# Second attention of a two-layer block: scores on two halves of TensorE's rows, and VectorE's steps without PSUM moved to GpSimd

## The chip, the cores and the metric

The kernel runs on one core of a Trainium2 chip, as one program. The metric is the device time of a whole execution in microseconds (us), the median over several runs. The engines are named PE (TensorE; its weight loads are PEld), DVE (VectorE), ACT (ScalarE), POOL (GpSimd) and SP (SyncE, which here issues most of the DMAs).

## The reference

The reference is two transformer layers on x of shape 32 x 256 x 128, each a sum of the stream, an attention and a feed-forward part. The change touches only the attention and the router of the second layer, which for one batch item (T = 256 tokens, C = 128) come to this:

```
Q, K, V = x @ wq, x @ wk, x @ wv                    # 16 heads of 8
local  = window attention, blocks of W = 32 queries, 2W = 64 keys, causal inside the window
GQ, GK, GV = x @ wgq, pool(x @ wgk), pool(x @ wgv)  # 8 latent heads, 64 pooled latents (4 tokens each)
rem    = softmax(GQ GK^T / sqrt(8), masked) @ GV @ r_out_w
out    = (sigmoid(Q gl) * local + sigmoid(Q gr) * rem) @ w_out
probs  = softmax(x @ gate_w); w, idx = top_8(probs); w = w / sum(w)   # router of the experts
```

## The kernel before, in words

The program goes through five stages: layernorm and first attention over 32 batches of 256 tokens, the first feed-forward part with tokens sorted by expert, then the second attention with the router, and last the experts. The stage of the second attention handles one batch (`Batch(pair, half)`, `.b` its number) at a time. Each engine has its own queue, written out by hand in a function `step1`, and runs it strictly in order; semaphores (`S[...]`) link the queues. Names in `step1`: `b` is the batch in work, `p` the one before, `n` the next, `m` the one after that. Buffers are double, so at any moment parts of four batches are under way.

For a batch the steps run as follows. POOL fetches rows of the first feed-forward result by an indirect DMA (`gather`), multiplies them by the gate and adds them to the stream (`stream1`), and normalises (`norm1`, which waits in its middle for DVE's mean and variance, `mean1`). PE transposes (`xt1`), ACT copies the transposed tile to SBUF (`xT1`). DVE sums four tokens at a time into the pooled latents (`pool_latents`), and ACT spreads them (`xp1`). PE makes queries, keys and router logits (`qk`), latent queries and keys (`latents`), values. ACT writes the queries and keys into masked layouts (`keys`, `latent_keys`).

The scores of a batch come in four groups g of two blocks each. For a group PE (`scores`) puts 12 score tiles of 64 columns into two PSUM banks, one for each block n: a bf16 matmul of the identity with a mask, and on top of it the fp32 scores, with all 128 rows of the array in use though each head group lives on 32 of them. DVE takes the maximum and subtracts it (`shift`), ACT takes the exponential (`soft`), DVE transposes 32 x 32 blocks (`turn`), PE multiplies by the values (`attend`). After the four groups ACT copies the sums of the exponentials (`dens`) and then the unnormalised rows out of PSUM (`attended`), DVE inverts the sums (`invert1`), POOL multiplies the rows by them (`normalise_rows`, semaphore `scaled`), DVE transposes them (`turn_rows`), PE multiplies the remote part by its weight (`remote`). In the next `step1`, with the batch now called `p`, DVE forms the two gated parts (`combine`, `at1` and `at2`) and their sum `aT`, PE multiplies by `w_out` (`project`), and DVE adds the result to the residual (`finish`).

The router runs beside it on DVE: the top eight logits (`route`), then the weights of the experts and the shared gate (`weigh`: mask, sum, reciprocal, `sgc`, product into `tab`), which SP writes out.

Of the kernel before, what the change touches and what calls it, by code (L numbers as in the profile page):

```python
# [33 lines left out]
def program(nc, a, out):  # L34
# [27 lines left out]
    with ctx:  # L62
# [21 lines left out]
        halfneg = sb("halfneg", [P, 2])  # L84
        zeros = sb("zeros", [P, C])
# [120 lines left out]
        xp = sb("xp", [P, 2, NL])  # L206
        vrow = sb("vrow", [P, 2, C])
# [18 lines left out]
        mxs = sb("mxs", [P, 2, 12])  # L226
        pr = sb("pr", [P, 2, 12 * NL])
# [75 lines left out]
        sh1_done sh_sb shd_ps av_ps rd_done rows_turned rem2_ps v_out v_in0 v_in1 rows_sb gate_ps gate_sb comb aT_done scaled x1_copied ao_ps r1_done res_done  # L303
# [21 lines left out]
        def _(sp):  # L325
# [70 lines left out]
            for k, w in enumerate(("wq", "wk")):  # L396
                sp.dma_start(wqk[:, k, :], a["L1_attn_" + w]).then_inc(S["w1_in"], 16)
                sp.dma_start(wgqk[:, k, 0:DL], a["L1_attn_" + ("wgq", "wgk")[k]]).then_inc(S["w1_in"], 16)
                sp.dma_start(gcol[:, k:k + 1], a["L1_attn_gate_" + ("local_w", "remote_w")[k]].rearrange("h (d o) -> (h d) o", o=1)).then_inc(S["w1_in"], 16)
# [129 lines left out]
        def _(pool):  # L529
# [13 lines left out]
            pool.memset(halfneg[:, :], -0.5)  # L543
            pool.memset(owr[:, :], 0.0).then_inc(S["zeroed"], 1)
# [196 lines left out]
            def clear():  # L741
# [7 lines left out]
                                 quadcol[:, 0:4 * 8:8].unsqueeze(1).to_broadcast([P, 4, 4]))  # L749
                pool.memset(cnt_all[:, 0:1], 0.0)  # L750
# [12 lines left out]
            def stream1(n):  # L763
# [6 lines left out]
                pool.wait_ge(S["x1_done"], n.b * 2 + 1)  # L770
# [17 lines left out]
            def norm1(n, prior):  # L788
# [17 lines left out]
            def normalise_rows(b):  # L806
                pool.wait_ge(S["rows_sb"], 2 * b.b + 3)
# [6 lines left out]
            gather(Batch(0, 0))  # L814
            gather(Batch(0, 1))
            clear()
            stream1(Batch(0, 0))
            norm1(Batch(0, 0), False)
            stream1(Batch(0, 1))
            norm1(Batch(0, 1), False)  # L820
            gather(Batch(1, 0))
            with pool.Fori(0, LOOP - 1) as i:
                for b in (Batch(i, 0), Batch(i, 1)):
                    stream1(b.next().next())
                    norm1(b.next().next(), True)
                    normalise_rows(b)
                    add_stream(b)
                    gather(b.next().next().next())
            stream1(Batch(LOOP, 0))
            norm1(Batch(LOOP, 0), True)  # L830
            normalise_rows(Batch(LOOP - 1, 0))
            add_stream(Batch(LOOP - 1, 0))
            gather(Batch(LOOP, 1))
            stream1(Batch(LOOP, 1))
            norm1(Batch(LOOP, 1), True)
            normalise_rows(Batch(LOOP - 1, 1))
            add_stream(Batch(LOOP - 1, 1))
            normalise_rows(Batch(LOOP, 0))
            add_stream(Batch(LOOP, 0))
            normalise_rows(Batch(LOOP, 1))  # L840
            add_stream(Batch(LOOP, 1))
# [32 lines left out]
        def _(dve):  # L874
# [293 lines left out]
            dve.wait_ge(S["w1_in"], 16 * 18)  # L1168
# [10 lines left out]
            def sums1(n):  # L1179
                dve.wait_ge(S["x1_done"], n.b * 2 + 2)  # L1180
# [15 lines left out]
            def pool_latents(n):  # L1196
                dve.wait_ge(S["tT_sb"], n.b + 1)
                dve.tensor_reduce(xp[:, n.half, :], xT1[:, n.half, :].rearrange("p (n k) -> p n k", k=CHUNK), AX.X,
                                  ALU.add).then_inc(S["xp_done"], 1)

            RSTEPS = 4

            def route(n):
# [5 lines left out]
                ins.then_inc(S["rstep"], 1)  # L1209
                dve.wait_ge(S["rstep"], n.b * RSTEPS + 1)  # L1210
# [7 lines left out]
            def weigh(n):  # L1218
                u = n.half
                dve.wait_ge(S["ex_done"], n.b + 1)  # L1220
                dve.wait_ge(S["M_done"], n.b + 1)
                dve.tensor_tensor(exl[:, :, :], exl[:, :, :], mb[:, u], ALU.mult).then_inc(S["rstep"], 1)
                dve.wait_ge(S["rstep"], n.b * RSTEPS + 2)
                dve.tensor_reduce(wsum[:, 0, :], exl[:, :, :], AX.X, ALU.add).then_inc(S["rstep"], 1)
                dve.wait_ge(S["rstep"], n.b * RSTEPS + 3)
                dve.reciprocal(wsum[:, 1, :], wsum[:, 0, :]).then_inc(S["rstep"], 1)
                dve.wait_ge(S["rstep"], n.b * RSTEPS + 4)
                dve.tensor_scalar(sgc[:, u, :], tsg[:, :], 0.5, 0.5, ALU.mult, ALU.add)
                dve.tensor_tensor(tab[:, u, :, C:C + E1], exl[:, :, :], wsum[:, 1, :].unsqueeze(2).to_broadcast([P, 2, E1]),
                                  ALU.mult).then_inc(S["tab_done"], 1)  # L1230
# [28 lines left out]
            def invert1(b):  # L1259
                dve.wait_ge(S["rows_sb"], 2 * b.b + 2)  # L1260
# [1010 lines left out]
```

## Time and profile before

| | |
|---|---|
| median of 3 runs | 1795.48 us (1791.98 to 1797.09) |
| the profiled execution | 1784.54 us, span 1782.8 us |
| TensorE's mean granted clock, share of full speed | 0.955 |
| busy, share of the span | PE 91%, DVE 64%, ACT 57%, POOL 47% |

The busy shares are means over the whole span. The second attention lies between 980 and 1614 us, and the views by stretch and by order of time, shown further down, are taken there. A row of the timeline gives start, duration, engine, line, operation, output and inputs with their shape, and how many instructions were merged; durations of neighbours on one engine overlap a little, so what an operation takes of its queue is the distance to the next start. One fp32 matmul shows as two records.

### The profile page before, as it was taken

The numbers are of one execution on the slowest core, as the hardware profiler recorded it, in microseconds if no ns is written. First come the engines' busy times: TensorE is split into PE (matmuls) and PEld (weight loads), VectorE is DVE, ScalarE is ACT, GpSimd is POOL, SyncE is SP. The second block draws the span as 40 slices with busy tenths as digits, with TensorE's granted clock in tenths as the row PEclk, the third lists the DMA queues.
The fourth block names the chain that finished last, engine by engine and source line by source line (L and its number), as shares of the span: only waits on it lengthen the run. The fifth ranks groups of instructions, "written<-read, shape, count | busy, mean of one in ns | idle before, by whom it ended". The sixth has DMA issues, their size and how long they took to land. (4 is left out here: it accounts for less than half of the span.)

```text
span 1782.8 us, 43704 instructions
## 1 busy us (share of the span) xinstructions
PE 1623.9 (91%) x13929; PEld 1198.6 (67%) x13931; DVE 1143.2 (64%) x2695; ACT 1007.7 (57%) x2546; POOL 832.5 (47%) x1413
## 2 busy tenths in 40 slices
PE   4799999999999999989996899999999999995883
PEld 4655555555555555547996688888888888884772
DVE  3356555555555555543443699999999999995661
ACT  3355555555555555543442677777777777762341
POOL 5235555555555555553444444444444444412664
PEclk9999999999999999999998799999999999996676
DMA  7412221222222212212221112112111111115444
GB/s 194 128 31 76 55 55 54 54 54 54 54 54 54 54 54 54 54 47 83 65 65 44 31 43 43 40 38 43 41 40 41 43 40 41 43 35 109 96 84 118
DMA packets 207886, 107.45 MB, mean 60 GB/s; under 512 B 102745, under 2 KB 196250, under 8 KB 207770
## 3 DMA queue, kind: packets, MB, share of 16 engines
q1 hardware_dynamic: 197594, 93.16, 20.9%
q0 software_dynamic: 10240, 13.64, 3.5%
q8 instruction: 27, 0.44, 0.1%
q14 instruction: 25, 0.20, 0.0%
HBM read 61.85 MB, written 40.16 MB: 57 GB/s over the span
## 5 line engine op out<-in xcount | busy, mean ns | idle before, releaser
L662 POOL TENSOR_SCALAR_AFFINE_SELECT probs<-probs 128x512 f32<-128x512 f32 x256 | 183.8, 742 | 157.4 <-ACT probs L1446 157.3
L899 DVE TENSOR_REDUCE mneg<-bankS 128x2 f32<-128x256 f32 x256 | 107.5, 420 | 215.1 <-PE bankS L1778 193.7
L1446 ACT ACTIVATE probs<-bankT 128x1024 f32<-128x1024 f32 x128 | 131.1, 1025 | 180.7 <-PE bankT L1798 180.7
L900 DVE TENSOR_REDUCE mneg<-bankS 128x2 f32<-128x512 f32 x256 | 174.6, 682 | 0.0
L1437 ACT ACTIVATE qT<-bankA,bd 128x256 f32<-128x256 f32 x256 | 107.7, 474 | 89.8 <-PE bankA L1760 89.8
L1760 PE MATMUL bankA<-xnT,wd 128*128 128x256 f32 x512 | 149.6, 416 | 0.0
L655 POOL CAST qb<-qT 128x256 bf16<-128x256 f32 x256 | 97.7, 400 | 95.2 <-ACT qT L1437 95.0
L1812 PE MATMUL bankB<-probs,vaug 128*64 128x512 f32 x512 | 140.2, 626 | 1.1 <-ACT yT L1453 1.0
L1795 PE MATMUL bankT<-qT,kT 37*128 37x512 f32 x512 | 136.7, 610 | 3.5 <-DMA qT<-mT 1.8
L1542 ACT ACTIVATE pe<-pr 128x768 f32<-128x768 f32 x128 | 108.2, 845 | 28.2 <-DVE pr L1240 26.0
L1246 DVE STREAM_TRANSPOSE pt<-pe 128x768 f32<-128x768 f32 x128 | 123.8, 967 | 0.4 <-ACT pe L1542 0.2
L1453 ACT COPY yT<-bankB 128x512 f32<-128x512 f32 x128 | 75.1, 587 | 82.7 <-PE bankB L1816 82.7
L1760 PEld LDWEIGHTS bankA<-xnT,wd 128*128 128x128 f32 x512 | 89.7, 195 | 37.1 <-issue 29.7
L1773 PEld LDWEIGHTS bankS<-rowneg,rowsel 64*128 64x128 bf16 x1024 | 35.7, 94 | 83.4 <-issue 44.8
L1798 PEld LDWEIGHTS bankT<-qT,kT 37*128 37x128 f32 x512 | 50.1, 188 | 61.2 <-issue 61.2
L1816 PEld LDWEIGHTS bankB<-probs,vaug 128*64 128x64 f32 x512 | 37.4, 139 | 74.6 <-issue 65.5
L725 POOL COPY probs<-wall 128x516 f32 x72 | 45.0, 625 | 84.2 <-DVE qT L1131 81.3
L784 POOL TENSOR_SCALAR rstd<-mv 128x2 f32<-128x2 f32 x32 | 7.2, 225 | 163.7 <-DVE mv L1193 163.7
L1773 PE MATMUL bankS<-rowneg,rowsel 64*128 64x128 bf16 x1024 | 74.3, 221 | 10.2 <-DVE mneg L900 5.4
L760 POOL DMA_INDIRECT yg<-ys_sorted,idx_g x64 | 65.6, 1025 | 36.9 <-POOL gate_g L756 26.7
L1955 PE MATMUL bankT<-wall,qT 128*128 x576 | 78.6, 280 | 0.1
L1816 PE MATMUL bankB<-probs,vaug 128*64 128x256 f32 x512 | 78.1, 384 | 0.0
(317 smaller groups left out, 4640.8 us busy)
## 6 DMA issues: line engine op xcount, KB each, us to landing
rzb<-reciprocals SPq DMA_DIRECT2D x128, 128.0 KB
yT<-yT SPq DMA_DIRECT2D x64, 128.0 KB
xtab<-tab SPq DMA_DIRECT2D x32, 192.0 KB, 2.0
xs_sorted<-zeros SPq DMA_DIRECT2D x1, 4608.0 KB, 19.2
qT<-xs_sorted SPq DMA_DIRECT2D x36, 128.0 KB, 2.1
ys_sorted<-qT SPq DMA_DIRECT2D x36, 128.0 KB, 1.8
value_rows<-vrow SPq DMA_DIRECT2D x32, 128.0 KB, 1.8
vx<-value_rows SPq DMA_DIRECT2D x256, 16.0 KB, 1.8
```

Source lines behind the costliest of these rows:

```text
L662: pool.affine_select(out=blocks, in_=blocks, compare_op=ALU.is_ge, fill=0.0, base=0, pattern=[[0, 4], [1, P]], channel_multiplier=-1).then ...
L899: dve.tensor_reduce(mneg[:, n.half, 0, :, j], bankS[:, :, 0:128], AX.X, ALU.max, negate=True)
L900: dve.tensor_reduce(mneg[:, n.half, 1, :, j], bankS[:, :, 128:384], AX.X, ALU.max, negate=True).then_inc(S["red_done"], 1)
L1246: dve.transpose(pt[:, g].rearrange("p k b g q -> p (k b g q)"), pe1[:, g % 2].rearrange("p k s q -> p (k s q)")).then_inc(S["tr_done"], 1)
L1437: act.activation(qT[:, n.half, j, :], bankA[:, k * T:(k + 1) * T], ACT.Identity, bias=bd[:, j:j + 1]).then_inc(S["q_sb"], 1)
L1446: act.activation(pT[:, g % 2].rearrange("p e j t -> p e (j t)"), bankT[:, 0:2, :], ACT.Exp, scale=SCALE0).then_inc(S["exp_done"], 1)
L1542: act.activation(pe1[:, g % 2].rearrange("p k s q -> p s k q"), pr[:, g % 2, :].rearrange("p (s k q) -> p s k q", k=2, q=W), ACT.Exp, scal ...
L1760: ins = pe.matmul(bankA[:, k * T:(k + 1) * T], wd[:, 2 * r + k, :, :].rearrange("p e l -> p (e l)"), xnT[:, n.half, :], start=True, stop=True)
L1773: pe.matmul(blocks, rowsel[HALVES[e], k, :], rowneg[HALVES[e], k, :].unsqueeze(1).to_broadcast([LP, 2, LP]), start=(k == 0), stop=False, s ...
L1795: pe.matmul(bankT[:, e, :], kT[KEYS[e], u, 0:P], qT[KEYS[e], u, 2 * g:2 * g + 2, :].rearrange("p j t -> p (j t)"), start=True, stop=True, ...
L1812: pe.matmul(bankB[HALVES[e], :], vaug[:, u, 0, :], pT[:, g % 2, e].rearrange("p j t -> p (j t)"), start=True, stop=False, skip_group_check ...
L1816: ins = pe.matmul(bankB[HALVES[e], :].rearrange("p (j t) -> p j t", t=T)[:, :, P:T], vaug[:, u, 1, :], pT1[:, g % 2, e], start=False, stop ...
```

## The change

It has two parts, both in the second attention.

On PE a group of scores is laid out anew: the two banks now hold not the two blocks but two halves of the array's rows (partitions 0 to 63 and 64 to 127), and every matmul contracts over 64 rows only. `pick1` and `masks` are new constants for the masks (built once by POOL and ACT), `wgqk` is loaded twice so that the latent queries and keys exist on both halves, and ACT copies the latent keys for four row groups instead of two (`gkm`). DVE, ACT and `attend` see the same shapes in another order.

From DVE's queue seven instructions for each batch go to POOL's: the pooling (one reduction becomes two additions, `xq` and `xp`), the reciprocal of `dens` (now a power with exponent -1, `recd`), the sum `aT` (`gated_sum`), and of the router's weights the mask, `sgc`, the reciprocal of the sum (again a power) and the product into `tab` (`weigh`, `weights`). The sum itself stays on DVE (`weight_sum`). POOL gets a `step1` of its own that fixes the order.

```diff
             def normalise_rows(b):
+                pool.wait_ge(S["rows_sb"], 2 * b.b + 2)
+                passed(pool)
+                pool.tensor_tensor(recd[:, :, :].rearrange("p s h -> p (s h)"), dens[:, :, :].rearrange("p s h -> p (s h)"),
+                                   minus[:, 0:1].to_broadcast([P, 4 * SL]), ALU.pow).then_inc(S["rd_done"], 1)
                 pool.wait_ge(S["rows_sb"], 2 * b.b + 3)
                 pool.wait_ge(S["rd_done"], b.b + 1)
...
+            def pool_latents(n):
+                pool.wait_ge(S["tT_sb"], n.b + 1)
+                passed(pool)
+                pairs = xT1[:, n.half, :].rearrange("p (m k) -> p m k", k=2)
+                pool.tensor_tensor(xq[:, :], pairs[:, :, 0], pairs[:, :, 1], ALU.add).then_inc(S["xp_done"], 1)
+                pool.wait_ge(S["xp_done"], n.b * 2 + 1)
+                pairs = xq[:, :].rearrange("p (m k) -> p m k", k=2)
+                pool.tensor_tensor(xp[:, n.half, :], pairs[:, :, 0], pairs[:, :, 1], ALU.add).then_inc(S["xp_done"], 1)
+
+            def gated_sum(b):
+                pool.wait_ge(S["comb"], b.b * 2 + 2)
+                passed(pool)
+                pool.tensor_tensor(aT[:, :], at1[:, :], at2[:, :], ALU.add).then_inc(S["aT_done"], 1)
+
+            def weigh(n):
+                u = n.half
+                pool.wait_ge(S["ex_done"], n.b + 1)
+                pool.wait_ge(S["M_done"], n.b + 1)
+                passed(pool)
+                pool.tensor_scalar(sgc[:, u, :], tsg[:, :], 0.5, 0.5, ALU.mult, ALU.add)
+                pool.tensor_tensor(exl[:, :, :], exl[:, :, :], mb[:, u], ALU.mult).then_inc(S["rstep"], 1)
+
+            def weights(n):
+                u = n.half
+                pool.wait_ge(S["rstep"], n.b * 3 + 2)
+                passed(pool)
+                pool.tensor_tensor(wsum[:, 1, :], wsum[:, 0, :], minus[:, 0:1].to_broadcast([P, 2]), ALU.pow).then_inc(S["rstep"], 1)
+                pool.wait_ge(S["rstep"], n.b * 3 + 3)
+                pool.tensor_tensor(tab[:, u, :, C:C + E1], exl[:, :, :], wsum[:, 1, :].unsqueeze(2).to_broadcast([P, 2, E1]),
+                                   ALU.mult).then_inc(S["tab_done"], 1)
+
+            def step1(b, p, n, m, k):
+                if n:
+                    pool_latents(n)
+                if m:
+                    stream1(m)
+                if p:
+                    gated_sum(p)
+                if n:
+                    weigh(n)
+                if m:
+                    norm1(m, True)
+                if n:
+                    weights(n)
+                if b:
                     normalise_rows(b)
                     add_stream(b)
+                if k:
+                    gather(k)
...
             def step1(b, p, n, m):
-                if n:
-                    pool_latents(n)
...
                 if n:
-                    weigh(n)
+                    weight_sum(n)
                 if b:
                     shared_gated(b)
                     shared_hidden(b)
-                    invert1(b)
...
+                s = (bankS, bankT)[g % 2]
+                half = [slice(DL * k, DL * (k + 1)) for k in range(2)]
+                passed(pe)
                 for k in range(2):
-                    n = 2 * g + k
-                    s = (bankS, bankT)[g % 2][:, k, :]
-                    pe.matmul(s[:, 0:4 * NL], identb[:, :], maskl[:, min(n, 1), :].unsqueeze(1).to_broadcast([P, 4, NL]), start=True, stop=False)
-                    pe.matmul(s[:, 0:4 * NL], qx[:, u, n].rearrange("p h q -> p (h q)"), km[:, u, :, n * W:n * W + 2 * W], start=False, stop=True)
-                    pe.matmul(s[:, 4 * NL:6 * NL], identb[:, :], maskr[:, n, :].unsqueeze(1).to_broadcast([P, 2, NL]), start=True, stop=False)
-                    ins = pe.matmul(s[:, 4 * NL:6 * NL], gqx[:, u, n].rearrange("p h q -> p (h q)"), gkm[:, u, :, :], start=False, stop=True)
+                    pe.matmul(s[:, k, 0:6 * NL], pick1[half[k]].rearrange("p h q -> p (h q)"), masks[half[k], g].rearrange("p s c -> p (s c)"),
+                              start=True, stop=False, skip_group_check=True)
+                for c in range(2):
+                    n = 2 * g + c
+                    for k in range(2):
+                        pe.matmul(s[:, k, c * 2 * NL:(c + 1) * 2 * NL], qx[half[k], u, n].rearrange("p h q -> p (h q)"),
+                                  km[half[k], u, 2 * k:2 * k + 2, n * W:n * W + 2 * W], start=False, stop=True, skip_group_check=True)
+                for k in range(2):
+                    ins = pe.matmul(s[:, k, 4 * NL:6 * NL], gqx[half[k], u, 2 * g + k].rearrange("p h q -> p (h q)"), gkm[half[k], u, :, :],
+                                    start=False, stop=True, skip_group_check=True)
```

How the change moves instructions, in the order of the queues. First GpSimd, where one `step1` ends and the next begins. Before, inside the loop (the rows ISA and REGISTER_ALU are waits and address arithmetic):

```order
L811 TENSOR_TENSOR rows<-rows,recd 128x384
L777 REGISTER_ALU
L779 ISA
L779 TENSOR_TENSOR res<-res,xa_all 128x256
L755 ISA
L755 COPY idx_g<-pos_all 128x2
L756 REGISTER_ALU
L756 COPY gate_g<-gate_all 128x2
L757 REGISTER_ALU
L760 DMA yg<-ys_sorted,idx_g 128x128 x2
L768 TENSOR_SCALAR yg<-yg,gate_g 128x128 x2
```

and now, at the same place of the program:

```order
L817 TENSOR_TENSOR recd<-dens,minus 128x48
L823 TENSOR_TENSOR rows<-rows,recd 128x384
L787 TENSOR_TENSOR res<-res,xa_all 128x256
L763 COPY idx_g<-pos_all 128x2
L764 COPY gate_g<-gate_all 128x2
L768 DMA yg<-ys_sorted,idx_g 128x128 x2
L830 TENSOR_TENSOR xq<-xT 128x128
L833 TENSOR_TENSOR xp<-xq 128x64
L776 TENSOR_SCALAR yg<-yg,gate_g 128x128 x2
L781 TENSOR_TENSOR xa_all<-xa_all,yg 128x256
L838 TENSOR_TENSOR aT<-at 128x256
```

The inversion of the sums stands ahead of the rows; the pooling stands behind the gather's DMAs, and the gated sum behind the whole of `stream1`.

Second, GpSimd's rows from the second half of a `step1` up to the normalising of the rows, as they are now:

```order
L845 TENSOR_SCALAR sgc<-tsg 128x2
L846 TENSOR_TENSOR exl<-exl,mb 128x128
L804 COPY tab<-xa_all 128x2x128
L792 TENSOR_SCALAR rstd<-mv 128x2
L794 TENSOR_TENSOR rstd<-rstd,halfneg 128x2
L810 TENSOR_SCALAR tab<-tab,mv,rstd 128x128 x2
L852 TENSOR_TENSOR wsum<-wsum,minus 128x2
L854 TENSOR_TENSOR tab<-exl,wsum 128x2x64
L817 TENSOR_TENSOR recd<-dens,minus 128x48
L823 TENSOR_TENSOR rows<-rows,recd 128x384
```

Of these ten, before, only `tab<-xa_all`, the two of `rstd`, `tab<-tab,mv,rstd` and `rows` stood there; the other five came from VectorE.

Third, TensorE, where a group of scores lies between the queries and keys (`bankB<-xT,wqk`) and the latents. Before:

```order
L2019 MATMUL bankA<-gw,xT 128x65 x2
L1993 MATMUL bankS<-maskl,identb 128x256
L1994 MATMUL bankS<-km,qx 128x256
L1995 MATMUL bankS<-maskr,identb 128x128
L1996 MATMUL bankS<-gkm,gqx 128x128
L1993 MATMUL bankS<-maskl,identb 128x256
L1994 MATMUL bankS<-km,qx 128x256
L1995 MATMUL bankS<-maskr,identb 128x128
L1996 MATMUL bankS<-gkm,gqx 128x128
L2027 MATMUL bankT<-xT,wgqk 128x256
```

and now:

```order
L2067 MATMUL bankA<-gw,xT 128x65 x2
L2035 MATMUL bankS<-masks,pick 128x384 x2
L2040 MATMUL bankS<-km,qx 128x128 x4
L2043 MATMUL bankS<-gkm,gqx 128x128 x2
L2075 MATMUL bankT<-xT,wgqk 128x256
```

Neighbouring matmuls now alternate between the two row halves and the two banks; the columns that they stream add up to the same number as before (768 in bf16 and 768 in fp32).

## Rows read from the trace of the kernel before

**Rows 1.** Busy time by stretch: us, PE, PEld, DVE, ACT, POOL, then granted clock, DMA

```profile
1100.00:1500.00 400.00, 388.51 (x4018) 327.57 (x4017) 370.89 (x796) 306.27 (x920) 181.84 (x293) 1.00 0.19 41
...
1600.00:1700.00 100.00, 73.20 (x574) 61.16 (x572) 65.04 (x208) 34.14 (x95) 42.65 (x37) 0.69 0.48 98
```

**Rows 2.** One line of GpSimd: count, duration ns, first and last start

```profile
L811 POOL TENSOR_TENSOR rows<-rows,recd x32: 851/854/859, 1018.1 to 1609.0; 128x384 f32<-128x384 f32 x32
```

**Rows 3.** Waits of 1100 to 1500 us: us in total, times, longest

```profile
DVE xp L1198 <- ACT xT L1547: 17.7, 21, 0.8
```

**Rows 4.** VectorE's groups, 1100 to 1500 us: busy us, mean ns

```profile
L1261 DVE RECIPROCAL recd<-dens 128x48 f32<-128x48 f32 x21 | 9.4, 446 | 0.0
L1275 DVE TENSOR_TENSOR aT<-at 128x256 f32<-128x256 f32 x21 | 8.9, 424 | 0.7
L1198 DVE TENSOR_REDUCE xp<-xT 128x64 f32<-128x256 f32 x21 | 8.8, 420 | 17.7 <-ACT xT L1547 17.7
```

**Rows 5.** VectorE's timeline in one batch

```profile
1200.52 0.31 DVE L1208 MAX8 mx<-lg 128x8 f32<-128x64 f32 x2
...
1204.31 0.97 DVE L1246 STREAM_TRANSPOSE pt<-pe 128x768 f32<-128x768 f32 x1
1205.20 0.20 DVE L1193 BATCH_NORM_AGGREGATE mv<-stats 128x2 f32<-128x6 f32 x2
...
1206.20 0.25 DVE L1222 TENSOR_TENSOR exl<-exl,mb 128x128 f32<-128x128 f32 x1
1206.48 0.29 DVE L1224 TENSOR_REDUCE wsum<-exl 128x2 f32<-128x128 f32 x1
...
1207.42 0.68 DVE L1252 SCALAR_TENSOR_TENSOR shT<-tsh,bankA 128x512 f32<-128x512 f32 x1
...
1218.48 0.41 DVE L1281 TENSOR_TENSOR res<-bankT,res 128x256 f32<-128x256 f32 x1
```

**Rows 6.** TensorE's timeline: a group of scores, project; and from the first attention

```profile
1207.20 0.28 PE L1993 MATMUL bankS<-maskl,identb 128*128 128x256 bf16 x1
...
1208.96 1.07 PE L2100 MATMUL bankB<-sdw,shT 128*128 128x128 f32 x8
...
1216.62 0.66 PE L2106 MATMUL bankT<-wo,aT 128*128 128x128 f32 x4
...
504.67 1.04 PE L1795 MATMUL bankT<-qT,kT 37*128 37x512 f32 x4
```

**Rows 7.** GpSimd's groups over the whole span: busy us, mean ns

```profile
L786 POOL TENSOR_TENSOR rstd<-rstd,halfneg 128x2 f32<-128x2 f32 x32 | 23.2, 724 | 2.7
L623 POOL TENSOR_TENSOR xrstd<-xvar,halfneg 128x8 f32<-128x8 f32 x8 | 13.4, 1670 | 0.7
L625 POOL TENSOR_TENSOR xshift<-xshift,xrstd 128x8 f32<-128x8 f32 x8 | 1.6, 202 | 0.6
```

**Rows 8.** GpSimd's timeline in one batch

```profile
1205.61 0.23 POOL L784 TENSOR_SCALAR rstd<-mv 128x2 f32<-128x2 f32 x1 [5.12 <-DVE mv L1193]
...
1206.85 1.58 POOL L802 TENSOR_SCALAR tab<-tab,mv,rstd 128x128 f32<-128x128 f32 x2 [0.21 <-POOL rstd L786]
...
1211.04 0.73 POOL L779 TENSOR_TENSOR res<-res,xa_all 128x256 f32<-128x256 f32 x1 [0.39 <-ACT res L1613]
...
1214.27 0.97 POOL L760 DMA_INDIRECT yg<-ys_sorted,idx_g  x1 [0.30 <-issue]
1216.95 1.20 POOL L768 TENSOR_SCALAR yg<-yg,gate_g 128x128 f32<-128x128 f32 x2 [1.72 <-DMA yg<-ys_sorted,idx_g]
1218.43 0.73 POOL L773 TENSOR_TENSOR xa_all<-xa_all,yg 128x256 f32 x1 [0.28 <-POOL yg L768]
```

**Rows 9.** ScalarE's timeline in one batch

```profile
1213.05 0.39 ACT L1551 COPY xpr<-xp 128x256 f32<-128x256 f32 x1
...
1217.00 0.85 ACT L1542 ACTIVATE pe<-pr 128x768 f32<-128x768 f32 x1
...
1222.42 0.47 ACT L1573 ACTIVATE cnt_all<-bankS,carry 64x256 f32 x1
```

More of the change, by code:

```diff
@@ L84, in program @@
         halfneg = sb("halfneg", [P, 2])
+        minus = sb("minus", [P, 1])
         zeros = sb("zeros", [P, C])
@@ L226, in program @@
         mxs = sb("mxs", [P, 2, 12])
+        pick1 = sb("pick1", [P, 4, W], BF16)
+        masks = sb("masks", [P, NB // 2, 6, NL], BF16)
         pr = sb("pr", [P, 2, 12 * NL])
@@ L543, in _ @@
             pool.memset(halfneg[:, :], -0.5)
+            pool.memset(minus[:, :], -1.0)
             pool.memset(owr[:, :], 0.0).then_inc(S["zeroed"], 1)
@@ L749, in clear @@
                                  quadcol[:, 0:4 * 8:8].unsqueeze(1).to_broadcast([P, 4, 4]))
+                pool.memset(pick1[:, :, :], 0.0)
+                pool.memset(masks[:, :, :, :], 0.0)
                 pool.memset(cnt_all[:, 0:1], 0.0)
@@ L829, in _ @@
[L829 to L840, printed above, removed]
@@ L841, in _ @@
-            add_stream(Batch(LOOP, 1))
+                if k:
+                    gather(k)
+            first, second = Batch(0, 0), Batch(0, 1)
+            gather(first)
+            gather(second)
+            clear()
+            stream1(first)
+            norm1(first, False)
+            stream1(second)
+            pool_latents(first)
+            weigh(first)
+            norm1(second, False)
+            weights(first)
+            gather(Batch(1, 0))
+            step1(first, None, second, Batch(1, 0), Batch(1, 1))
@@ new lines, in _ @@
+            step1(second, first, Batch(1, 0), Batch(1, 1), Batch(2, 0))
+            with pool.Fori(1, LOOP - 1) as i:
+                step1(Batch(i, 0), Batch(i, 0).before(), Batch(i, 1), Batch(i + 1, 0), Batch(i + 1, 1))
+                step1(Batch(i, 1), Batch(i, 0), Batch(i + 1, 0), Batch(i + 1, 1), Batch(i + 2, 0))
+            step1(Batch(LOOP - 1, 0), Batch(LOOP - 2, 1), Batch(LOOP - 1, 1), Batch(LOOP, 0), Batch(LOOP, 1))
+            step1(Batch(LOOP - 1, 1), Batch(LOOP - 1, 0), Batch(LOOP, 0), Batch(LOOP, 1), None)
@@ L1216, in route, with weight_sum @@
                 dve.tensor_tensor(mb[:, u], lg1[:, :, 0:E1], lgr[:, :, :], ALU.not_equal).then_inc(S["M_done"], 1)
[L1218 to L1223, printed above, removed]
-                dve.tensor_reduce(wsum[:, 0, :], exl[:, :, :], AX.X, ALU.add).then_inc(S["rstep"], 1)
[L1225 to L1230, printed above, removed]
+            def weight_sum(n):
+                dve.wait_ge(S["rstep"], n.b * 3 + 1)
+                passed(dve)
+                dve.tensor_reduce(wsum[:, 0, :], exl[:, :, :], AX.X, ALU.add).then_inc(S["rstep"], 1)
             def shift(b, g):
@@ L1257, in shared_hidden @@
                 dve.tensor_tensor(h, h, bank[1][:, :], ALU.mult).then_inc(S["sh_sb"], 1)
-            def invert1(b):
-                dve.wait_ge(S["rows_sb"], 2 * b.b + 2)
-                dve.reciprocal(recd[:, :, :], dens[:, :, :]).then_inc(S["rd_done"], 1)
             def turn_rows(b):
@@ L1582, in latent_keys @@
                 spread(gqx[:, n.half], bank[2][:, 0:T])
-                for g in range(2):
+                for g in range(4):
                     q = slice(W * g, W * g + W)
-                    ins = act.copy(gkm[q, n.half, g, :], bank[2][q, 256:256 + NL])
+                    ins = act.copy(gkm[q, n.half, g % 2, :], bank[2][q, 256:256 + NL])
                 ins.then_inc(S["gk_sb"], 1)
@@ L1662, in _ @@
             act.wait_ge(S["wprep"], 1)
+            for k in range(2):
+                q = slice(DL * k, DL * k + W)
+                act.copy(pick1[q, :, :], identb[q, q].unsqueeze(1).to_broadcast([W, 4, W]))
+                act.copy(masks[q, 0, 0:2, :], maskl[q, 0, :].unsqueeze(1).to_broadcast([W, 2, NL]))
+                act.copy(masks[q, 0, 2:4, :], maskl[q, 1, :].unsqueeze(1).to_broadcast([W, 2, NL]))
+                for g in range(1, NB // 2):
+                    act.copy(masks[q, g, 0:4, :], maskl[q, 1, :].unsqueeze(1).to_broadcast([W, 4, NL]))
+                for g in range(NB // 2):
+                    ins = act.copy(masks[q, g, 4:6, :], maskr[q, 2 * g + k, :].unsqueeze(1).to_broadcast([W, 2, NL]))
+            ins.then_inc(S["l1_consts"], 1)
             xt1(Batch(0, 0))
```

53 lines of the change are left out of this document (20 added, 33 removed).

## The prediction

> **What bounds the kernel now.** I read the busy times by stretch first, then one batch of the second attention on each queue in order of time. In the stretch from 1100 to 1500 us TensorE is busy for 388.5 of 400 us and VectorE for 370.9, GpSimd only for 181.8 [rows 1]. One line of GpSimd runs once a batch, from 1018.1 to 1609.0 us in 32 executions [rows 2], so a batch takes (1609.0 - 1018.1) / 31 = 19.06 us, and 400 us hold 21 of them. Per batch that is 18.5 us of TensorE, 17.7 of VectorE and 8.7 of GpSimd. The list of waits shows one for VectorE worth naming: 17.7 us in 21 batches, 0.84 each, for the transposed tile ahead of the pooling [rows 3]. So VectorE and TensorE bound this stage together, and GpSimd looks half free. That view misleads in one respect: GpSimd's queue is strictly in order, and what counts for this change is where in it the new work stands and how long its slowest item is.
>
> **TensorE's part.** A group of scores takes 1208.96 - 1207.20 = 1.76 us now [rows 6], four of them 7.0 us a batch. Do matmuls on two row halves run side by side? In the first attention four records of 512 fp32 columns with 37 rows, two on each half, take 1.04 us together. Eight records of 128 columns with all rows take 1.07 [rows 6], 0.13 each, so four of 512 one after the other would take about 2.1. They do overlap. The new group streams the same 768 bf16 and 768 fp32 columns as the old, half of them on each row half, so I take half of 1.76, 0.9 us; if nothing overlapped it stays at 1.76. TensorE's batch falls from 18.5 to 15.0 us, or not at all. I take the former, by the row with that layout.
>
> **VectorE's part.** Removed per batch: the reciprocal 0.45, the sum 0.42, the pooling 0.42 [rows 4], and of the 1.22 us from `exl` to the shared part (1206.20 to 1207.42) all but the sum's 0.29 [rows 5], 0.93. Together 2.2 us, and the wait of 0.84 goes with the pooling. VectorE's own work would be about 15.5 us a batch.
>
> **GpSimd's part: the prices.** A power is dear there. `pow` on 128x2 takes 724 ns, on 128x8 1670 ns, while an ordinary two-input operation on 128x8 takes 202 [rows 7]. The slope is (1670 - 724) / 6 = 158 ns for each element of a partition. The new `recd<-dens,minus` has 48 of them: 724 + 46 x 158 = 7.98 us, for VectorE's 0.45. Bounds: not below 1.67 us, the row with 8 elements, and not above 10.0 us (six times that row). I take 8.0, since both rows have the same form (the second with the same broadcast exponent). The rest: `wsum` as `pow` on 128x2, 0.72; plain two-input operations between the 0.20 of 128x8 and the 0.73 of 128x256 [rows 7, 8]: `aT` 0.73, `xq` 0.46, `xp` 0.32, `exl` and `tab` 0.46 each; `sgc` 0.23 as `rstd` on two columns. Sum of added work: 8.0 + 0.72 + 0.73 + 0.78 + 0.92 + 0.23 = 11.4 us. With the 8.7 of before GpSimd is busy 20.1 us a batch, over the 19.06 that a batch takes now, before any wait.
>
> The Trainium skill (GPSIMD Engine Reference, 3 Performance versus the Vector engine) gives about 2.6 cycles an element at 1.2 GHz for a two-input operation; the plain rows agree (529 ns for 248 elements, 2.1 ns each). Applied to the power it would make `recd` an estimated 0.3 us and the sum of added work 3.7; the power's rows are 70 times dearer per element, and they decide. That is the rival B below.
>
> **The walk through the queues.** I set t = 0 where GpSimd ends the rows of batch b (`scaled`) and go round to the same point of the next batch. Every step is a distance in a row of before unless said.
> GpSimd: `res` 0.73, to 0.8; then the indices and the two DMAs of the gather, from 1211.77 to 1215.24 in rows 8, 3.5 us, to 4.3 [rows 8]; the pooling, new at this place, 0.46 + 0.1 + 0.32, to 5.2. The fetched rows land 1.7 us after the second DMA (1216.95 - 1215.24), at 6.0; `stream1` takes 1216.95 to 1219.16, to 8.2 [rows 8]; only now the gated sum, 0.73, to 9.0. VectorE had delivered its inputs at about 3.2. TensorE's `project` waits for it: 0.66 [rows 6], to 9.65; VectorE's `finish`, 0.41 [rows 5], to 10.1. VectorE arrives there at 5.9, so it stands still for 3.8 us.
> ScalarE meanwhile: `xp1` waits for the pooling at 5.2. From the start of `xpr` to the end of the exponential of group 1 are 4.8 us (1213.05 to 1217.85), to 10.0 [rows 9]: the same moment. Queued behind that are `latent_keys` and everything else on ScalarE.
> VectorE: `turn` 0.9, to 11.0; router, statistics and `shift` of group 3, 1200.52 to 1204.31, 3.8, to 14.8; `turn` and `mean1`, 1.0, to 15.8 [rows 5]. Its last `turn` waits for the exponential of group 3: ScalarE needs 5.0 us from the end of one exponential to the end of `cnt_all` (1217.85 to 1222.89) [rows 9] and 0.4 more for two added copies, 15.4, and 0.85 for the exponential, 16.3; the turn ends at 17.2.
> GpSimd from `mean1` on: 0.2 until it starts, 1205.61 to 1208.43 for the normalising, 3.0 together, to 18.8 [rows 8]; `wsum` and `tab` 0.72 + 0.1 + 0.46, to 20.1; `recd` 8.0, to 28.1 (its input came at 18.4); `rows` 0.1 + 0.85, to 29.05 [rows 2].
> So a batch takes 21.1 us plus the price of `recd`: 29.05 with 8.0. VectorE, which in its queue goes from the shared part and `shift(n, 0)` to `turn_rows`, is ready for that at about 20.8 and waits 8 us; behind it stands the whole next batch. SP's `save_table` comes at 20.1, and behind it only the counts, the stream and the next values, which are needed a batch later.
> The clock: TensorE would be busy 15.0 of 29 us, half the time. In the stretch with TensorE busy for 73% the granted clock is 0.69 of full speed, against 1.00 in rows with 97% [rows 1]. At 1.2 GHz for part of the batch `project` and the last `attend` groups on this path take up to 1.1 us longer; I add 0.5. That gives 29.5 us a batch, with 29.05 and 30.2 as its ends.
> Other costs: two more DMAs of small weights at the start, hidden below the first attention; the memset of `masks` (about 1.5 us) once, ScalarE's 20 copies once, below the wait for the first tile.
>
> **The sum.** (29.5 - 19.06) x 31 = 324. The first batch pays its `recd` too, 8; the last two gaps have neither stream, normalising nor gather and cost about 9 each in place of 10.4, -3; the memset 1.5. Together +330 us on the profiled execution of 1784.5: 2115. The median of the runs lies 11 us higher, so 2125.
>
> **Rivals.**
> A, the forecast: the long power stands in a loop through GpSimd's queue; 2125. Chance 0.75, its own range 2060 to 2190 (slope 15% off either way is 1.2 us a batch, the clock 0.6, the walk 0.5).
> B, the power is cheap (0.3 to 1.7 us, by the page's rule or because its cost flattens), the loop stays: 21.4 to 22.8 us a batch, +2.3 to +3.7, 73 to 115 us: 1870 to 1910. For it: nothing in the rows with 8 elements. Against: the slope. 0.06.
> C, GpSimd is the bound by its work but the loop leaves slack, or the power grows less than linearly: 22 to 26 us a batch, 1890 to 2010. Its busy 20.1 plus 0.9 of waiting inside the gather and 1.0 of small gaps is the floor of 22. 0.07.
> D, the other side: the power costs under 1 us and the gated sum doesn't hold up `project`, as GpSimd gets to it by 6 rather than 9; then VectorE's 15.5 us of work plus about 1 of waits set the batch, 16.5, and (16.5 - 19.06) x 31 = -79: 1715. It decides once the loop is under 19.06, so it needs both. If the row halves did not overlap, TensorE's 18.5 would leave only -17. For it: GpSimd is idle for over half of the stage now [rows 1]. 0.09.
> E, no change within 0.3%, which is about what a measurement of this kernel can tell: B and D cancelling, 0.03.
>
> **How the numbers follow.** Predicted is A's. A's range holds 0.7 of the chance; to leave out no more than 0.2 the range goes down over C to 1890 and up to 2195. Faster is D, same E, slower A, B and C, 0.88.
>
> **What would show it.** Right: `recd` at 7 to 9 us on GpSimd; GpSimd busy for two thirds or more of the stage; VectorE's largest wait at `rowsT` for `rows`, the next at `res` for TensorE's project; a group of scores in 0.8 to 0.9 us; a granted clock under 1. Wrong: `recd` under 2 us, which takes the forecast to B or D, or `aT` done within 6 us of `rows`.

## The result, and the profile after

| | before | after |
|---|---|---|
| median | 1796.28 us (4 runs) | 2112.65 us (4 runs, 2102.81 to 2114.09) |
| ratio | | 1.175 (95% interval 1.171 to 1.180) |
| profiled span | 1782.8 us | 2112.3 us |
| mean granted clock | 0.955 | 0.875 |

The changed kernel is 17.5% slower. The prediction was 2125 us (1890 to 2195). First the line that runs once a batch, as in [rows 2], and above it the new instruction; these two and later rows of one line give count, duration (shortest/median/longest, ns), first and last start:

```profile
L817 POOL TENSOR_TENSOR recd<-dens,minus x32: 8004/8011/8015, 1032.8 to 1926.2; 128x48 f32<-128x48 f32 x32
...
L823 POOL TENSOR_TENSOR rows<-rows,recd x32: 851/851/852, 1041.0 to 1934.4; 128x384 f32<-128x384 f32 x32
```

The power on 48 elements takes 8.01 us each time. A batch takes (1934.4 - 1041.0) / 31 = 28.82 us, for 19.06 before. So the spans differ by 9.76 x 31 = 303 us between the first and the last batch, 22.9 us ahead of the first `rows` and 4.1 behind the last: together the 329.5 by which the spans differ. Of the 22.9 us, 12.5 lie ahead of the stage, where the change adds only two small loads of weights: the first gather begins at 979.1 us here and at 966.6 in the profile of before, at 968 to 976 in all others of this study (at 975.5 in experiment 3, which lacks those loads). The rest is mostly the first power, 8.0, and the memsets of the new constants, 1.5.

The 31 gaps are not alike: the first 29 average 29.1 us, and the last two, in which nothing is left to fetch or to normalise, take 25.6 and 23.9.

The busy times by stretch (us, PE, PEld, DVE, ACT, POOL, then clock, DMA), to be held against [rows 1]:

```profile
1200.00:1600.00 400.00, 254.13 (x2772) 215.33 (x2771) 220.12 (x425) 205.02 (x626) 272.58 (x304) 0.82 0.13 27
```

GpSimd is now the busiest engine with 68%, and still idle for a third; VectorE and TensorE, which bounded the stage, are busy for 55 and 64%. No engine is full: that is the sign of a loop that goes through several queues, one waiting for the next. The list of waits of the same stretch names its links:

```profile
ACT xpr L1582 <- POOL xp L833: 159.2, 14, 11.8
...
PE bankT L2140 <- DVE rowsT L1301: 116.8, 14, 8.7
DVE rowsT L1301 <- POOL rows L823: 113.4, 14, 8.4
POOL sgc L845 <- ACT tsg L1622: 76.0, 14, 5.5
DVE mxs L1276 <- PE bankS L2043: 32.3, 27, 2.1
DVE res L1315 <- PE bankT L2154: 25.7, 13, 2.4
```

ScalarE waits 11.4 us a batch for GpSimd's pooling, VectorE 8.1 for GpSimd's rows, and TensorE, behind VectorE, 8.3; and GpSimd itself waits 5.4 us for ScalarE. Now GpSimd's queue in order of time, from the end of one batch's rows (1303.22 + 0.85 = 1304.07) to the next:

```profile
1303.22 0.85 POOL L823 TENSOR_TENSOR rows<-rows,recd 128x384 f32<-128x384 f32 x1 [0.17 <-POOL recd L817]
...
1307.24 0.95 POOL L768 DMA_INDIRECT yg<-ys_sorted,idx_g  x1 [0.30 <-issue]
...
1308.70 0.29 POOL L833 TENSOR_TENSOR xp<-xq 128x64 f32<-128x64 f32 x1
1309.96 1.20 POOL L776 TENSOR_SCALAR yg<-yg,gate_g 128x128 f32<-128x128 f32 x2 [0.97 <-DMA yg<-ys_sorted,idx_g]
...
1312.13 0.73 POOL L838 TENSOR_TENSOR aT<-at 128x256 f32<-128x256 f32 x1
1318.25 0.19 POOL L845 TENSOR_SCALAR sgc<-tsg 128x2 f32<-128x2 f32 x1 [5.39 <-ACT tsg L1622]
...
1320.17 0.23 POOL L792 TENSOR_SCALAR rstd<-mv 128x2 f32<-128x2 f32 x1 [0.99 <-DVE mv L1249]
...
1324.11 8.01 POOL L817 TENSOR_TENSOR recd<-dens,minus 128x48 f32<-128x48 f32 x1
1332.29 0.85 POOL L823 TENSOR_TENSOR rows<-rows,recd 128x384 f32<-128x384 f32 x1 [0.17 <-POOL recd L817]
```

Counted from 1304.07: pooling done at 4.9 us, gated sum at 8.8, the power starts at 20.0, the rows end at 29.1. Between the gated sum and the mask of the router GpSimd stands still for 5.4 us: idle time that it can't use, since everything further on in its queue waits for that chain through TensorE, VectorE and ScalarE.

TensorE's group of scores, between `project` and the values, in the same batch:

```profile
1312.91 0.71 PE L2154 MATMUL bankT<-wo,aT 128*128 128x128 f32 x4 [1.43 <-POOL aT L838]
1313.56 0.34 PE L2035 MATMUL bankT<-masks,pick 64*128 64x384 bf16 x2
1313.73 0.61 PE L2040 MATMUL bankT<-km,qx 64*128 64x128 f32 x8
1314.18 0.39 PE L2043 MATMUL bankT<-gkm,gqx 64*128 64x128 f32 x4
1314.49 0.71 PE L2090 MATMUL bankB<-wv,xT 128*128 128x128 f32 x4
```

It takes 1314.49 - 1313.56 = 0.93 us, for 1.76 in [rows 6]: the two row halves do run side by side. So do three of the four groups of this batch; the first one after TensorE's wait of 8.6 us for `rowsT` takes 1.72 (1308.35 to 1310.07), at the lower clock.

### The profile page after: what moved, and what is told of

Read it like the earlier page. It is cut to its first block and busy times, and to the rows that moved or that the text cites. A ratio compares the mean times of both kernels' runs of the same rounds, so it can differ in the third digit from the quotient of the medians.

```text
span 2112.3 us, 44607 instructions
## 1 busy us (share of the span) xinstructions
PE 1633.4 (77%) x14185; PEld 1207.1 (57%) x14187; DVE 1086.8 (51%) x2471; ACT 1025.7 (49%) x2630; POOL 1183.5 (56%) x1672
## 5 line engine op out<-in xcount | busy, mean ns | idle before, releaser
L817 POOL TENSOR_TENSOR recd<-dens,minus 128x48 f32<-128x48 f32 x32 | 256.4, 8011 | 10.8 <-ACT dens L1655 10.8
L2140 PE MATMUL bankT<-rowsT,wro 128*128 128x128 f32 x128 | 39.2, 461 | 263.2 <-DVE rowsT L1301 263.2
L2140 PEld LDWEIGHTS bankT<-rowsT,wro 128*128 128x128 f32 x128 | 29.8, 324 | 270.7 <-DVE rowsT L1301 270.7
L1582 ACT COPY xpr<-xp 128x256 f32<-128x256 f32 x32 | 13.0, 405 | 340.4 <-POOL xp L833 340.4
L1301 DVE STREAM_TRANSPOSE rowsT<-rows 128x384 f32<-128x384 f32 x32 | 18.5, 578 | 256.2 <-POOL rows L823 256.2
L1573 ACT ACTIVATE pe<-pr 128x768 f32<-128x768 f32 x128 | 108.0, 844 | 13.5 <-DVE pr L1280 10.7
L845 POOL TENSOR_SCALAR sgc<-tsg 128x2 f32<-128x2 f32 x32 | 6.2, 193 | 180.6 <-ACT tsg L1622 180.6
L1276 DVE TENSOR_REDUCE mxs<-bankS 128x12 f32<-128x768 f32 x64 | 61.3, 957 | 77.2 <-PE bankS L2043 77.2
```

Of the source, the lines that this page charges most:

```text
L817: pool.tensor_tensor(recd[:, :, :].rearrange("p s h -> p (s h)"), dens[:, :, :].rearrange("p s h -> p (s h)"), minus[:, 0:1].to_broadcast( ...
L1573: act.activation(pe1[:, g % 2].rearrange("p k s q -> p s k q"), pr[:, g % 2, :].rearrange("p (s k q) -> p s k q", k=2, q=W), ACT.Exp, scal ...
```

## The experiments

**1. The 48 reciprocals back on VectorE.** Everything else stays as changed.

```diff
             def normalise_rows(b):
-                pool.wait_ge(S["rows_sb"], 2 * b.b + 2)
-                passed(pool)
-                pool.tensor_tensor(recd..., dens..., minus[:, 0:1].to_broadcast([P, 4 * SL]), ALU.pow).then_inc(S["rd_done"], 1)
                 pool.wait_ge(S["rows_sb"], 2 * b.b + 3)
...
                     shared_hidden(b)
+                    invert1(b)
```

> The changed kernel with one step undone: the 48 reciprocals go back to VectorE's queue, everything else as changed. Theory (loop through GpSimd's queue): the 8.0 us of the power go out of the loop, but GpSimd still reaches the rows only 20.0 us after the previous ones, so a batch takes 20.9 to 21.3 us, and the kernel stays slower than before: 1796 + 2.0 x 31 = about 1860 us (1850 to 1875). Rival (the power alone is to blame): VectorE's work sets the batch, 16.5 to 17.5 us, 1715 to 1750 us.

Measured: 1899.26 us, ratio to before 1.059 (1.057 to 1.061).

```profile
L819 POOL TENSOR_TENSOR rows<-rows,recd x32: 852/856/857, 1027.7 to 1723.6; 128x384 f32<-128x384 f32 x32
```

A batch takes 22.45 us. Taking the power out gives back 6.4 of the 9.76 us lost, and without it the kernel is still slower than before, so the rival falls. But the theory's figures, 20.9 to 21.3 us and 1850 to 1875, are 1.2 us a batch and 24 us short. The trace shows what it left out, in GpSimd's rows of one batch:

```profile
1321.68 0.40 POOL L850 TENSOR_TENSOR tab<-exl,wsum 128x128 f32<-128x128 f32 x1
1322.72 0.86 POOL L819 TENSOR_TENSOR rows<-rows,recd 128x384 f32<-128x384 f32 x1 [0.64 <-ACT rows L1661]
```

GpSimd is ready at 1322.08 and waits 0.64 us for ScalarE's copies of the rows, which follow the sums by some 2.1 us; under the 8 us of the power these copies had been hidden, and the prediction's walk had not named them. The second part is TensorE's clock. The groups of `project` from 1200 to 1500 us, first of the changed kernel, mean of a record 300 ns:

```profile
L2154 PE MATMUL bankT<-wo,aT 128*128 128x128 f32 x40 | 7.1, 300 | 17.3 <-POOL aT L838 17.3
```

and of this one, 461 ns, the longer duration of the lower clock:

```profile
L2155 PE MATMUL bankT<-wo,aT 128*128 128x128 f32 x52 | 15.9, 461 | 22.4 <-POOL aT L834 22.4
```

Four records take 1.22 us instead of 0.71, and VectorE's `finish` ends 10.7 us after the rows where it ended at 10.1; GpSimd is ready 0.4 us later than by the walk. This batch takes 22.0 us and is the shortest kind: in the stage the batches go round in threes of 22.0, 22.9 and 23.4 us, and GpSimd's wait for the copies is 0.6, 1.6 and 2.0 us in them. Why they go in threes was not looked into.

**2. The new scores alone**, on the kernel before: `masks`, `pick1`, the second load of `wgqk`, the two added copies of `gkm`, `scores` and the order in `attend`, with GpSimd's and VectorE's queues as they were.

> The kernel before with the new layout of the scores alone (masks, TensorE, the two added copies), GpSimd and VectorE untouched. Theory: VectorE's queue bounds the batch at 17.7 us of work and the wait of 0.84 us for the transposed tile, which lies behind two groups of scores, goes away: 18.0 to 18.3 us a batch, 1765 to 1772 us. Rival 1 (TensorE was the bound): 3.5 us a batch less, about 1690 us. Rival 2 (VectorE bounds and nothing of its waits depends on the scores): within 0.3% of 1796 us.

Measured: 1774.92 us, ratio 0.990 (0.988 to 0.993).

```profile
L816 POOL TENSOR_TENSOR rows<-rows,recd x32: 851/854/859, 1026.7 to 1598.6; 128x384 f32<-128x384 f32 x32
```

A batch takes 18.45 us, 0.61 less than before. The busy times of 1200 to 1500 us tell who bounds it:

```profile
1200.00:1500.00 300.00, 259.82 (x3219) 217.32 (x3219) 286.19 (x621) 245.26 (x750) 142.97 (x228) 1.00 0.19 42
```

TensorE has fallen to 87%, VectorE has risen to 95%. VectorE's wait ahead of the pooling is 0.31 us where it was 0.84. Of TensorE's 3.3 us a batch the stage gives back about what VectorE no longer waits (0.53 of the 0.61 us). The theory's mechanism holds, its figure (1765 to 1772) is 3 us too low.

**3. The move to GpSimd alone**, with the scores as before.

> The kernel before with the move to GpSimd alone, scores as before. Theory: the loop runs through GpSimd and TensorE has room enough: a batch of 28.8 to 29.6 us, 2105 to 2135 us, within 1% of the changed kernel. Rival (the halves give back several us a batch also now): over 2160 us.

Measured: 2099.17 us, ratio 1.171 (1.168 to 1.173), a batch of (1926.2 - 1035.4) / 31 = 28.74 us. That is within 1% of the changed kernel, and 6 us under the 2105 to 2135 expected. The whole loss is in this part, and with the loop in place the new scores give nothing: the changed kernel's batch is 28.82 us, and its ratio of 1.175 (1.171 to 1.180) is not below this one. The changed kernel's granted clock is the lower of the two, 0.82 for 0.87 in the stretch from 1300 to 1500 us, with TensorE busy for 64 and 70% of it.

**4. The price of a power.** Seven powers with exponent -1 are added once, ahead of the second attention:

```diff
                 pool.memset(carry[:, :, :], 0.0).then_inc(S["pads"], 16)
+                for k, w in enumerate((2, 8, 16, 24, 32, 48, 64)):
+                    pool.tensor_tensor(probe_o[:, k, 0:w], probe_i[:, 0:w], probe_e[:, 0:1].to_broadcast([P, w]), ALU.pow)
```

> The kernel before with seven powers added once on GpSimd ahead of the second attention, exponent -1, on 2, 8, 16, 24, 32, 48 and 64 elements a partition; their outputs are used by nothing. Theory (linear): 0.41 us + 0.158 us an element: 0.72, 1.67, 2.94, 4.2, 5.5, 8.0 and 10.5 us. Rival (fixed cost that flattens, or dear only on 48 elements with real sums): 48 elements under 6 us here.

The groups of GpSimd (busy us, mean ns):

```profile
L758 POOL TENSOR_TENSOR probe_o<-probe_i,probe_e 128x64 f32<-128x64 f32 x1 | 10.5, 10510 | 0.0
L758 POOL TENSOR_TENSOR probe_o<-probe_i,probe_e 128x48 f32<-128x48 f32 x1 | 8.0, 7992 | 0.0
L758 POOL TENSOR_TENSOR probe_o<-probe_i,probe_e 128x32 f32<-128x32 f32 x1 | 5.4, 5406 | 0.0
L758 POOL TENSOR_TENSOR probe_o<-probe_i,probe_e 128x24 f32<-128x24 f32 x1 | 4.1, 4146 | 0.0
L758 POOL TENSOR_TENSOR probe_o<-probe_i,probe_e 128x16 f32<-128x16 f32 x1 | 2.9, 2885 | 0.0
L758 POOL TENSOR_TENSOR probe_o<-probe_i,probe_e 128x8 f32<-128x8 f32 x1 | 2.0, 2024 | 0.0
...
L758 POOL TENSOR_TENSOR probe_o<-probe_i,probe_e 128x2 f32<-128x2 f32 x1 | 0.8, 835 | 0.0
```

From 16 to 64 elements the slope is (10510 - 2885) / 48 = 159 ns, from [rows 7] it was 158. In this range the cost is linear, and on 48 elements it is nearly the same for a constant 2.5 here and real sums in the kernel (7992 and 8011 ns). The two smallest, which run first, are dearer than the line and than [rows 7] (0.84 and 2.02 us for 0.72 and 1.67); why was not tested, and nothing here rests on them. The run took 1821.84 us.

**5. The power on half of the sums.** The other 24 are copied, so half of the rows are not normalised.

```diff
+                half = 4 * SL // 2
+                pool.tensor_copy(recd...[:, half:2 * half], dens...[:, half:2 * half])
-                pool.tensor_tensor(recd..., dens..., minus[:, 0:1].to_broadcast([P, 4 * SL]), ALU.pow).then_inc(S["rd_done"], 1)
+                pool.tensor_tensor(recd...[:, 0:half], dens...[:, 0:half], minus[:, 0:1].to_broadcast([P, half]), ALU.pow).then_inc(S["rd_done"], 1)
```

> The changed kernel with the power on 24 of the 48 sums; the other 24 are copied as they are, so half of the rows are not normalised. Theory: recd takes 4.15 us by the run of single powers and the copy 0.2, so 3.7 us less in the loop of every batch: 31 x 3.7 = 115 us less than the changed kernel, 1995 to 2005 us. Rival (something else holds the loop at over 28 us): 2080 us or more.

Measured in one run: 1987.23 us, and a batch of 25.15 us, from the first and last start of

```profile
L825 POOL TENSOR_TENSOR rows<-rows,recd x32: 849/849/850, 1031.8 to 1811.4; 128x384 f32<-128x384 f32 x32
```

That is 3.67 us less than 28.82, and the power on 24 elements (4.16 us in this trace) with the copy (0.20) takes 3.65 less than 8.01, or 3.85 without the copy. So what is taken off the power comes off the batch in full. The time is 8 us under the 1995 to 2005 expected, in a single run.

**6. GpSimd's queue in another order**, all moved work, the power too, left on GpSimd.

```diff
                 if n:
                     pool_latents(n)
-                if m:
-                    stream1(m)
                 if p:
                     gated_sum(p)
+                if m:
+                    stream1(m)
+                if k:
+                    gather(k)
                 if n:
                     weigh(n)
...
                     add_stream(b)
-                if k:
-                    gather(k)
```

> The changed kernel with GpSimd's step written in another order: pooling, gated sum, stream1, gather, router's mask, norm1, weights, rows, residual. All moved work, the power of 48 elements included, stays on GpSimd. Theory: of the loop 21.1 us + 8.0, the detour over gather and stream1 ahead of the pooling and the sum goes (about 4.5 us), so a batch takes 24.4 to 24.9 us by the walk: 1960 to 1980 us. Rival (the batch is set by GpSimd's total work, the order is worth nothing): over 2080 us.

Measured: 2051.59 us, ratio 1.145 (1.140 to 1.150), a batch of 27.04 us. The order is worth 1.8 us here and not 4.5: the rival, over 2080 us, is refuted by 28 us, but the batch is 2.1 to 2.6 us longer than the theory's 24.4 to 24.9. A part of that is in ScalarE's queue. The rows end at 1308.05 here:

```profile
1309.50 0.40 ACT L1582 COPY xpr<-xp 128x256 f32<-128x256 f32 x1 [8.20 <-POOL xp L833]
1311.68 0.37 ACT L1592 COPY qs<-bankB 128x256 f32<-128x256 f32 x1 [1.78 <-PE bankB L2063]
```

With the pooling early, ScalarE waits for the next thing, TensorE's new queries. They are late because `remote(b)` stands ahead of them in TensorE's queue and waits for the rows, and with them for the power. In the changed kernel the same delay lay below the detour over the gather.

**7. TensorE's remote part behind the next queries**, on the kernel of experiment 6.

```diff
             def step1(b, p, n, m):
                 if n:
                     qk(n, b is not None)
+                if p:
+                    remote(p)
                 if b:
                     scores(b, 2)
...
-                if b:
-                    remote(b)
...
+            remote(Batch(LOOP, 1))
             project(Batch(LOOP, 1))
```

> The kernel of the run order_only (all work on GpSimd as changed, its step in the new order) with TensorE's remote part moved from the end of its step to behind the next batch's queries, keys and logits. Theory (in that run TensorE stood at the remote part, waiting for the late rows, with the next queries and keys queued behind): they are now made while the power runs, ScalarE's chain starts at the pooling, 1.7 us earlier, so 25.3 to 25.6 us a batch for 27.0: 1996 to 2010 us for 2052. Rival (GpSimd's own work or VectorE's wait for the scores holds the batch at 27): 2045 us or more.

Measured: 2014.80 us, ratio 1.127 (1.124 to 1.130), a batch of (1835.7 - 1037.4) / 31 = 25.75 us. The gap is where the theory put it: 1.3 of the 1.7 us come back. The time is 5 us over the 1996 to 2010 expected, and the 0.9 us by which the batch is still longer than the 24.9 of experiment 6's theory were not followed further.

**8. The same move on the changed kernel**, as a control.

> The changed kernel with only TensorE's remote part moved behind the next queries and keys, GpSimd's order as changed. Theory: there the pooling behind the gather comes 4.9 us after the rows and the queries and keys already 3.5 us after them, so nothing waits for them: within 0.5% of the changed kernel, a batch of 28.8 us. Rival (TensorE's place was part of the loss there too): 1% or more faster than it.

Measured: 2121.88 us, a batch of (1940.8 - 1036.6) / 31 = 29.17 us. Nothing is gained, so the rival falls, and TensorE's place in the loop matters only once the detour is gone. But the ratio is 1.187 (1.184 to 1.190), 1% above the changed kernel's, and the batch 0.35 us longer, where no difference was expected. `project` shows why:

```profile
L2154 PE MATMUL bankT<-wo,aT 128*128 128x128 f32 x40 | 12.2, 461 | 9.5 <-POOL aT L838 9.5
```

461 ns a record again, at a mean granted clock of 0.74 in the stretch from 1200 to 1500 us for 0.83. TensorE makes its queries earlier, idles ahead of the latents (1.9 us of waiting for `xpr`), and the slow part then covers `project`, which VectorE waits for: 4.3 us each time for 2.0 in the changed kernel.

**9. Power back and queue reordered**, experiments 1 and 6 together.

> The changed kernel with the 48 reciprocals back on VectorE and GpSimd's step in the new order (pooling, gated sum, stream1, gather first). Theory (power and order are the two causes and add up): the loop falls to about 17.5 us a batch, VectorE's queue is then full: 1740 to 1755 us, faster than the kernel before and than the new scores alone (1775). Rival (GpSimd's queue still delays VectorE elsewhere, or the clock falls again): 1790 to 1860 us.

Measured: 1766.03 us, ratio 0.984 (0.979 to 0.989), a batch of (1589.8 - 1028.8) / 31 = 18.10 us. The two causes explain the loss and a little more: the kernel is faster than before, and in the traces than the new scores alone by 0.35 us a batch (the intervals of the two ratios just touch). The expected 17.5 us are missed by 0.6, and 1755 us by 11.

The two causes do not simply add up, as the expectation had it. The new order is worth 28.82 - 27.04 = 1.8 us with the power in the queue and 22.45 - 18.10 = 4.35 us without it, and the latter is about what the walk gives for the detour. TensorE's clock accounts for a part. ScalarE is held up by the queries behind the remote part here too, but by 0.54 us where it was 1.78 in experiment 6:

```profile
1303.54 0.37 ACT L1593 COPY qs<-bankB 128x256 f32<-128x256 f32 x1 [0.54 <-PE bankB L2064]
```

The queries' matmuls from 1200 to 1500 us, first in experiment 6, where TensorE comes to them after a wait of 8.6 us, then here, after one of 0.7:

```profile
L2063 PE MATMUL bankB<-xT,wqk 128*128 128x256 f32 x44 | 21.1, 634 | 0.0
```

```profile
L2064 PE MATMUL bankB<-xT,wqk 128*128 128x256 f32 x64 | 17.2, 392 | 0.0
```

From the end of the rows to the copy of the queries (`qs`) it was 1311.68 - 1308.05 = 3.63 us there and is 1303.54 - 1301.15 = 2.39 here. So 1.2 of the 1.78 us that ScalarE waited in experiment 6 are the lower clock that follows the long wait for the power.

**10. The same with the remote part moved (experiment 7) and `add_stream` behind the pooling.**

```diff
                 if n:
                     pool_latents(n)
                 if p:
+                    add_stream(p)
                     gated_sum(p)
...
                     normalise_rows(b)
-                    add_stream(b)
```

> The kernel of the run recd_back_order with the remote part behind the next queries and keys, and GpSimd's addition to the residual behind the next pooling. Theory: the loop through ScalarE shrinks by about 1.1 us a batch, from 18.1 to 17.0 to 17.3, where VectorE's 16.6 us of queue nearly fill it: 1733 to 1745 us, ratio 0.968 to 0.975. Rival (ScalarE's queue alone, 15 us of work and the wait for the last attend, holds the batch at 18): 1760 us or more.

Measured five times: 1746.80 us, ratio 0.977 (0.974 to 0.979).

```profile
L819 POOL TENSOR_TENSOR rows<-rows,recd x32: 852/854/860, 1029.9 to 1571.3; 128x384 f32<-128x384 f32 x32
...
1200.00:1500.00 300.00, 268.93 (x3458) 229.31 (x3458) 277.52 (x549) 255.78 (x786) 201.84 (x361) 1.00 0.21 45
```

A batch takes 17.46 us, 1.6 less than before, close above the 17.0 to 17.3 expected (and 2 us above the 1733 to 1745). What each of the two added moves is worth by itself was not measured. This version is the fastest of the study, 2.3% faster than the kernel before: only cheap steps on GpSimd, the pooling and the gated sum ahead of the gather, and the 48 reciprocals left on VectorE. VectorE (93%), TensorE (90%) and ScalarE (85%) are now nearly even.

## Why the prediction was right

**The price of the power** (8.0 us, the step on which all hung): measured 8.01, and linear from 16 to 64 elements by experiment 4. The rate that the Trainium skill gives for two-input operations (GPSIMD Engine Reference, 3 Performance versus the Vector engine, about 2.6 cycles an element at 1.2 GHz) agrees roughly with the moved additions, 0.29 us for `xp` on 64 elements and 0.72 for `aT` on 256, which is 2.2 ns an element; it doesn't hold for the power, at 159 ns.

**The walk through the queues.** Held against the rows after, from the end of one batch's rows: pooling done at 4.9 us (forecast 5.2), gated sum 8.8 (9.0), start of the power 20.0 (20.1), end of the rows 29.1 (29.05). The first 29 gaps average 29.1, and all 31 with the two short last ones 28.82. Experiment 5 confirms that the power stands in the loop (3.67 us come back for the 3.65 taken off it), and experiment 1 that most of it does: 6.4 of its 8.0 us come back before the next path, ScalarE's copies, takes over. Experiments 6 and 9 show that the order of the queue is a cause of its own, and experiment 3 that nothing of the loss comes from the scores.

**What the order costs** was not a number of the prediction, but its walk suggests the 4.5 us that the expectation of experiment 6 took from it, and that was 2.7 too much as long as the power stayed (1.8 measured), and about right without it (4.35). The walk followed the one path that came last and said nothing of the next: TensorE's queries behind `remote`, 1.3 us by experiment 7, and in experiment 1 ScalarE's copies of the rows, hidden until then below the power.

**The clock.** The forecast added 0.5 us a batch for it and gave 29.5, where the 29 full gaps measure 29.1: in the changed kernel the term was worth little. The granted clock did fall, to 0.82 in the stretch shown, but TensorE's slow part comes right after its long wait: in the batch shown its first matmuls after it are slow, and at `project`, 8 us later, it is back at 0.71 us. VectorE did wait for the slow scores (2.3 us a batch, `mxs`), longer than for `project` (1.9, `res`), which the prediction had named as its second wait; that `mxs` cost nothing, because `finish` behind it was late anyway, is read from the order of the rows and was not tested. In experiments 1 and 8 the slow part reached `project`, and there it cost some 0.4 us a batch; in experiment 6 it reached the queries, for 1.2.

**TensorE's part**: 0.93 us a group for 0.9 forecast, at the full clock; the first group of a batch, 1.72, had not been foreseen. **VectorE's part** was worth nothing in the changed kernel, and rival D, the only faster one, needed a cheap power and an early sum; experiments 9 and 10 put the sum early and, in place of a cheap power, the 48 reciprocals back on VectorE, and reached 1766 and 1747 us, not 1715. In experiment 10 VectorE works 16.15 of the 17.46 us (D had 15.5 of 16.5, without the 0.45 of the reciprocals) and stands idle for 1.3; in experiment 9 it waits 0.8 us a batch for ScalarE's exponentials, a queue that D had left out.

**The sum**: 330 us forecast on the profiled execution, 329.5 measured. That it agrees so closely is luck. The batches gave 303 where 324 less the 3 of the last two gaps were forecast, and 12.5 us of the rest lie ahead of the stage, where the profiled executions differ with no known cause. In medians the rise is 316 us, and the forecast of 2125 is 12 too high; that is the size of its error.

## What to carry to other kernels

Before moving work to an engine that looks idle, price each instruction at its new size from two rows of that engine, not from its price on the old one: a power on GpSimd cost 18 times VectorE's reciprocal. Then write down what stands ahead of it in the in-order queue; here a gather of 3.5 us and a wait for its data delayed a 0.7 us addition on which three engines depended. When no engine is full after a change, look for a loop through several queues, walk it once round, and note the second-latest arrival at each join too, for it is what you will meet after the first repair. For the same reason what a repair is worth depends on the others: here the same reordering gave 1.8 us with the power in place and 4.35 without it.

## What the runs showed of the hardware

A power on GpSimd costs 159 ns for each further element of a partition between 16 and 64: 2.9 us for 16, 8.0 for 48, 10.5 for 64. Two row halves of TensorE's array stream fp32 and bf16 matmuls side by side: a group of scores of 1.76 us takes 0.93.

The clock granted to TensorE can't be read off its busy share: it was 1.00 with 90 and 87% busy (experiments 10 and 9), 0.87 with 70% (experiment 3), 0.82 with 64% (the changed kernel), but 0.80 with 74% (experiment 7) and 0.74 with 70% (experiment 8). In the batches looked at the slow matmuls come behind a wait of TensorE, of 8.6 us in the changed kernel, of about 2 us in experiment 1, of 4.7 and of 1.9 us in experiment 8; behind one of 1.9 us in experiment 9 they were not slow. Nor does the mean tell the cost: in the changed kernel the low clock fell on matmuls that did not lengthen the loop, in experiments 1 and 8 on `project` (461 ns a record for 300), in experiment 6 on the queries (634 for 392). In experiment 8 an earlier place for TensorE's work went with a kernel that is 1% slower.
